# Row normalisations moved from VectorE to ScalarE, with a bias term made by GpSimd, and new instruction orders

## What is computed

```python
h = _layernorm(x) * (1 + ca) + sa              # block 0
x = x + ga * linear_attention(h)               # 16 heads of 8, elu + 1
h = _layernorm(x) * (1 + cb) + sb
xn = _layernorm(h) * gamma + beta
x = x + gb * (h + top2_of_8_experts(xn))       # 128 -> 512 -> gelu -> 128
h = _layernorm(x) * (1 + ca) + sa              # block 1
x = x + ga * softmax_attention(_layernorm(h))  # 8 heads of 16
h = _layernorm(x) * (1 + cb) + sb
x = x + gb * (h + chosen_of_8_experts(h))      # one 128 x 128 matrix each
```

## Time and profile before

| | |
|---|---|
| Median of the three runs | 684.64 us |
| Lowest and highest of them | 679.55 and 1851.92 us |
| The profiled execution's own time | 681.48 us |
| Its span in the profile | 679.7 us |
| Mean granted TensorE clock | 0.978 |
| PE busy | 607.0 us (89%), 3838 matmuls |
| DVE busy | 494.6 us (73%), 1298 instructions |
| ACT busy | 388.1 us (57%), 859 |
| POOL busy | 329.9 us (49%), 363 |
| DMA | 106.42 MB, mean 157 GB/s |

### The profile page before, as it was taken

The page is one execution under the profiler, slowest core; times in us unless marked ns, Lnnn a source line. Parts: engine busy times, 40 slices in busy tenths (PEclk is TensorE's granted clock), DMA queues, the critical chain, the costliest instruction groups (busy, mean ns, idle before and its releaser), DMA issues. The chain is left out here.

```text
span 679.7 us, 12016 instructions
## 1 busy us (share of the span) xinstructions
PE 607.0 (89%) x3838; PEld 386.7 (57%) x3838; DVE 494.6 (73%) x1298; ACT 388.1 (57%) x859; POOL 329.9 (49%) x363
## 2 busy tenths in 40 slices
PE   8889899999898899789999998888998987999974
PEld 4556558889888788566245598332344324533332
DVE  4778889931686635677868843898998872889897
ACT  2334136888656567347788666665665475555610
POOL 5203378155277767521883431448265464054623
PEclk9999999999899999989999999998999999879999
DMA  8300315777789986986488776118321829321012
GB/s 334 114 0 1 108 44 176 238 231 229 233 268 307 311 291 215 276 272 150 156 198 251 177 270 230 43 40 197 65 32 47 152 77 203 106 63 46 17 31 63
DMA packets 47422, 106.42 MB, mean 157 GB/s; under 512 B 7440, under 2 KB 22608, under 8 KB 45824
## 3 DMA queue, kind: packets, MB, share of 16 engines
q1 hardware_dynamic: 41808, 94.82, 47.1%
q0 software_dynamic: 5120, 10.50, 5.4%
q10 hardware_dynamic: 432, 0.34, 0.2%
...
## 5 line engine op out<-in xcount | busy, mean ns | idle before, releaser
L874 ACT ACTIVATE bufa<-PS 128x512 f32<-128x512 f32 x256 | 140.8, 599 | 68.0 <-PE PS L1565 58.2
L1206 DVE TENSOR_REDUCE mxs<-PS 128x2 f32<-128x1024 f32 x128 | 151.7, 1220 | 38.3 <-PE PS L1549 37.3
L833 ACT ACTIVATE bufb<-PS,bufb 128x128 f32<-128x128 f32 x368 | 103.5, 382 | 52.5 <-PE PS L1514 52.1
L1514 PE MATMUL PS<-bufb 128*128 128x128 f32 x736 | 98.8, 282 | 15.9 <-ACT bufb L841 6.2
L1514 PEld LDWEIGHTS PS<-bufb 128*128 128x128 f32 x736 | 90.9, 195 | 25.1 <-issue 10.7
L1522 PE MATMUL PS<-bufb 128*128 128x128 f32 x736 | 95.5, 276 | 1.5 <-ACT bufb L833 1.5
L689 POOL DMA_INDIRECT slots_in<-bufb x64 | 65.1, 1017 | 61.1 <-DVE bufb L1152 42.7
L1522 PEld LDWEIGHTS PS<-bufb 128*128 128x128 f32 x736 | 89.2, 192 | 5.7 <-ACT bufb L833 3.5
L1565 PE MATMUL PS<-stk 108*128 108x512 bf16 x256 | 85.1, 391 | 8.1 <-ACT bufa L874 6.4
L1549 PE MATMUL PS<-stk 96*128 96x512 bf16 x256 | 80.4, 402 | 7.8 <-DVE mxs L1206 4.8
L700 POOL DMA_INDIRECT bufb<-slots_out,bufb x64 | 62.4, 976 | 48.4 <-issue 33.3
...
## 6 DMA issues: line engine op xcount, KB each, us to landing
...
```

The costliest lines, as they stand in the source:

```text
L833: last = nc.scalar.activation(hs[:, n % HR, fc, :], ps[:, P * fc:P * fc + P], ACT.Gelu_apprx_tanh, bias=ws[:, n % WR, F + fc:F + fc + 1])
L874: nc.scalar.activation(probs[:, i % PR, j, :], psum("s2", i, j), ACT.Exp, scale=DH1 ** -0.5)\
L1206: nc.vector.tensor_reduce(mxs[:, gr % 2, 2 * j:2 * j + 2, h], psum("s1", i, j).rearrange("p (c n) -> p c n", c=2), axis=AX.X, op=ALU.max)\
L1514: last = nc.tensor.matmul(ps[:, P * fc:P * fc + P], ws[:, n % WR, P * fc:P * fc + P], xq[:, q % 2, P * x:P * x + P], start=True, stop=True)
```

## The change

Each `normalise` becomes a ScalarE activation, `Identity(x * scale + bias)`, with scale = `rstd` and bias = -mean * `rstd`. The mean is kept negated (a factor -0.5 in place of 0.5), and GpSimd makes the bias by one multiply more after the power. VectorE's statistics of the next pair now wait for ScalarE's normalisation of this one.

```diff
-            own.count(nc.gpsimd.memset(scales[:, :, 0], 0.5))
+            own.count(nc.gpsimd.memset(scales[:, :, 0], -0.5))
...
-                    tt(d, d, mhalf[:, :], ALU.pow).then_inc(rstd_ready[kind], 1)
+                    own.link(tt(d, d, mhalf[:, :], ALU.pow))
+                    tt(m[:, :, 0], m[:, :, 0], d, ALU.mult).then_inc(rstd_ready[kind], 1)
...
+            def normalise(kind, i, src, dst, done, lo=0, hi=NT):
+                n = NORMS.index(kind)
+                a.wait_ge(rstd_ready[kind], i + 1)
+                for t in range(lo, hi):
+                    last = nc.scalar.activation(dst[:, t, :], src[:, t, :], ACT.Identity, bias=mom[:, n, t, 0:1],
+                                                scale=rstd[:, n, t:t + 1])
+                last.then_inc(done, 1)
...
+                if kind == "an2":
+                    if i:
+                        a.wait_ge(a_oT, i)
+                        a.wait_ge(a_x, i)
+                    normalise("an1", i, tiles(X, i), za, a_z)
+                if kind == "bnn":
...
+                    normalise("bn1", i, tiles(X, i), hb[i], b_n)
+                if kind == "bn4":
+                    if i:
+                        a.wait_ge(sc_out, 256 * i)
+                    normalise("bn3", i, hb[i], z2, b_z)
...
                 if i:
-                    v.wait_ge(rstd_ready[kind], i)
+                    v.wait_ge(normed[kind], i)
...
-                own.count(nc.vector.tensor_scalar(m[:, :, 0], m[:, :, 0], 0.5, None, ALU.mult))
+                own.count(nc.vector.tensor_scalar(m[:, :, 0], m[:, :, 0], -0.5, None, ALU.mult))
...
-            def normalise(kind, i, src, dst, done, lo=0, hi=NT):
-                n = NORMS.index(kind)
-                v.wait_ge(rstd_ready[kind], i + 1)
-                if kind in OWN_NORMS:
-                    own.wait()
-                for t in range(lo, hi):
-                    last = nc.vector.tensor_scalar(dst[:, t, :], src[:, t, :], mom[:, n, t, 0:1],
-                                                   rstd[:, n, t:t + 1], ALU.subtract, ALU.mult)
...
+            normed = {"an1": a_z, "bn1": b_n, "bn3": b_z, "cn1": c_n2, "cn3": c_z, "dn1": d_z}
...
-                    normalise("bn1", i, tiles(X, i), h, None)
+                    v.wait_ge(b_n, i + 1)
```

The steps an2, bn4, cn2, cn4, dn2 and dl2 go from DVE's list to ACT's, and `bnn` is new there. All five lists are also written out in another order; two lines of POOL's show the kind of difference:

```diff
-        bga.3.0 bga.3.1 bga.3.2 bga.3.3 cn1.3.0 fin.0.0 cn2.3.0 dn1.0.0 cn3.3.0 dmo.0.0 fin.1.0 dn1.1.0 dmo.1.0 cpt.6.0 rsc.0.0
-        rsc.0.1 rsc.0.2 rsc.0.3 cpt.7.0 fin.2.0 dn1.2.0 rga.0.0 rga.0.1 dx.2.0 rga.0.2 dx.2.2 rga.0.3 dx.2.4 dx.2.6 en1.0.0
+        bga.3.0 bga.3.1 bga.3.2 bga.3.3 cn1.3.0 fin.0.0 cn2.3.0 dn1.0.0 cn3.3.0 dmo.0.0 cpt.6.0 fin.1.0 dn1.1.0 cpt.7.0 dmo.1.0
+        rsc.0.0 rsc.0.1 rsc.0.2 rsc.0.3 fin.2.0 dn1.2.0 rga.0.0 rga.0.1 rga.0.2 rga.0.3 dx.2.0 en1.0.0 dx.2.2 dx.2.4 dx.2.6
```

335 lines of the change are left out of this document (161 added, 174 removed).

## The result

| | before | changed |
|---|---|---|
| median of 3 runs | 684.64 us | 693.07 us |
| lowest and highest | 679.55 and 1851.92 us | 686.93 and 696.73 us |
| the profiled execution | 681.48 us | 693.07 us |
| its span | 679.7 us | 691.3 us |

The changed kernel is slower by a little, clear of the interval though less than 2%: 1.0166 of before, 95% interval 1.0107 to 1.0225. A second measurement (after_b) gave 1.0154 (1.0112 to 1.0196), 694.72 against 685.3 us. The forecast was 677 us, a gain of 1.1%.

The account below looks back on a forecast made before the run. TensorE was taken to bound the middle, a chain of small steps over all engines the start, VectorE the tail. Profiled 681.5 + 3 - 7 - 2 = 675.5, plus 2 for unnamed gaps, gave 677 us, range 664 to 694.

Parts of the forecast that it names:

- The start: Up to the first expert tile: about +3 us, range 0 to +6, with that tile near 109.5.
- (a) to (c): Start: slower bnn.0 step 0.8 us plus multiply 0.3; statistics about 5 us late; `z2` step 1.1 more, ending near 64.
- I count half of the delay back: Start: VectorE's list holds four steps less, 8.6 us, so half of `z2`'s almost 6 us delay returns; scatter near 82.
- (b), the place of the statistics: Start: VectorE does phi(q) of pair 1 ahead of pair 0's statistics, which start about 5 us late.
- (a) The store: Middle: store byo.2.1 goes ahead of nine stack loads, removing TensorE's 5.39 us gap before 290.75; -5.5 us with some clock.
- rival 3: Nothing gained from the moved DMAs, as bandwidth limits transfers and the gap comes elsewhere: 684.5 us, chance 0.28.
- (b) cpt.7.0: Middle, last layer's first slots: terms go before the scatter; -3.5 of 5 us, 2.0 clock and 3 gap.
- (c) Steps among the exponentials: Middle: five ScalarE steps each stall TensorE perhaps 1 us, 3 us back from sooner maxima: +2; steps before gelus covered.
- rival 1: ScalarE's in-order list blocks and each step shows on TensorE nearly in full: 27 us in the middle, 700.5 us, chance 0.12.
- (d) What no one could name: Middle: new lists may open a gap elsewhere; counted as nothing there, 6 us kept for the range.
- The tail: Last attention result to last add, VectorE busy nearly throughout: two half steps leave it; about -2 us, -4 to +1.
- three conditions for "wrong": First expert tile before 106, TensorE's waits for exponentials past 12 us in total, or a new middle gap over 4 us.

Follow-up runs that it names:

- three_moves_c: Changed kernel with pair 0's statistics before VectorE's query part, one ScalarE normalisation four gelu groups later, one expert tile's weights before nine stack loads: 695.88 us, 1.0213 of before.
- byo_only: Kernel before with one word moved, SP's store byo.2.1 ahead of the nine stack loads: 683.33 us, 1.0011 of before.
- before_dma_c: Kernel before with store byo.2.1 ahead of the nine stack loads and GpSimd's copy cpt.7.0 ahead of the 16 scatters: 697.38 us, 1.0220 of before.
- late_on_dve: Changed kernel with three attention normalisation steps (cn2.3.0, dn2.0.0, cn4.3.0) back on VectorE: 707.05 us, 1.0336 of before.
- split_only: Changed kernel's code with the orders of before, normalisations on ScalarE where VectorE had begun them: 833.45 us, 1.0591 of before, on a chip of the slower kind.
- order_only_b: Changed kernel's orders with all 25 normalisation steps back on VectorE, GpSimd still making the bias: 732.75 us, 1.0658 of before.
- mid_and_tail: Changed kernel with before's order on TensorE and VectorE between score tiles 16 and 23 and in the tail: 821.66 us, 1.0343 of before, slower kind of chip.

## Why the prediction was wrong, step by step

**The durations.** The step of 8 takes 3.18 to 3.21 us, not 2.9; the estimate of 3.2 from the Trainium skill (ScalarE: Activation LUTs, What ACT_TABLE_LOAD costs) was right and mine low. All steps fill 76.6 us of ScalarE, not 67. That its total still came to 448.6 (forecast 448) is luck: the rest of its work fills 8 us less than before. VectorE has 431.3 (forecast 444): it lost 63 us and not 51, 58.7 of them the steps, of which two were stretched (5.48 and 5.76 us), and I counted all at 2.14. The table loads are 15, as forecast. No normalisation is stretched.

**The start, +3 forecast, +5.4 at the first expert group (0 to +6 held it).** (a) to (c) were right: `z2` ends at 65.07 (forecast 64). The step that was too kind is "I count half of the delay back": 6.7 us at `z2` are still 6.2 at the scatter and 5.4 at 111.85 (in after_b 6.4, 4.0 and 4.3). three_moves_c shows that (b), the place of the statistics, was 3.3 to 4.4 us of it. In the end the start mattered less than its size: the lead that three_moves_c won there was gone by exponential 65.

**The middle, -7 forecast.** From the first gelu to the last exponential it took 535.7 us before (110.6 to 646.3) and 535.7 after (117.3 to 653.0): 0, inside -14 to +8, but made of other sums.

- (a) The store, -5.5 forecast. The cause of the gap was right (byo_only), the gain was not: a wait for the stack loads and the clock take it back (683.33 against 683.02 us). In the changed kernel the weights behind the same nine loads were late, and a gap of 5.90 us opened one tile later. This is rival 3 (its reason, the bandwidth, was not tested), and **the step that failed is to count a gap of 5.39 us as 5.5 us of gain** without asking what is late next: undone alone it gave 0 (1.0011, 0.9983 to 1.0040).
- (b) cpt.7.0, -3.5 forecast. Between exponentials 193 and 256 the change gains 8.0 us: 1.8 of the wait and the rest of it mostly clock. Before lost 7.01 x 0.28 + 9.33 x 0.07 + 9.75 x 0.25 + 9.96 x 0.09 = 6.0 us to it from 570 to 610, the change nothing. The forecast had 3.5 for the wait and the first of these four stretches. But byo_only, with the orders of before there and a wait of 2.71 us, lost only 6.94 x 0.14 + 9.45 x 0.03 + 9.46 x 0.12 + 9.81 x 0.05 = 2.9 us in the same 40 us, so some 3 of the 8 are where the falls happened to lie, and on kind B this stretch is 10 us longer with the new orders (92.1 to 93.5 against 82.0). No run takes this move alone out of the changed kernel: that it is the move's gain is likely, not shown. In the kernel before it costs: 12 us in this stretch, 15 in the whole (before_dma_c).
- (c) Steps among the exponentials, +2 forecast. They cost no more than forecast: TensorE's waits for exponentials (L1565) are 8.2 us in the whole program, 6.4 before. The 3 us that I gave back "for the maxima that come sooner" didn't come: the waits for maxima (L1549) went from 4.8 to 7.4. Yet exponentials 97 to 193 come 3.8 us sooner, and VectorE would have done worse (late_on_dve). The steps among the gelus, "covered by TensorE's lead" and put at nothing, are **the step of the middle that failed**: TensorE's waits for gelus grew by 5.9 us from the first gelu to exponential 33 (2.8 to 8.7), in a stretch that is 9.5 us longer. The 3.67 us before 239.85 are their clearest piece. Beside them stand 3.2 us more of waits for expert weights and, in return, 5.7 less for the copies and 2.1 less for slots; the rest is unused matmuls, small waits and the clock. The split alone loses 9 us there too (split_only, on kind B), but so do the orders without it (19 in order_only_b, on kind A); how the 9.5 divide between the two is not shown. It is rival 1's mechanism at a third of its price or less.
- (d) What no one could name was 4.6 us between exponentials 65 and 97, in many waits of half a microsecond, where no normalisation falls. It comes with the new order (order_only_b) and goes with the old one (mid_and_tail, on kind B).

**The tail, -2 forecast, +4.9 measured**, outside -4 to +1. ScalarE's step was as cheap as forecast: from the last of the statistics to the next transposes it is 3.4 us (666.92 to 670.32), where it was 5.2 (655.62 to 660.86). **What failed is that I put the tail down to VectorE's work alone** and did not look at fil.3.1, which the new order of TensorE puts behind a dense tile. The row order of the two lists would have shown it. With the old order there the tail is 35.9 us in place of 38.4 to 38.8 (mid_and_tail, kind B), so this place is about half of the loss; where the rest comes from is open.

So the sum is +6.7 (first gelu) + 0 + 4.9 = 11.6 us, where +3 - 7 - 2 = -6 was forecast, and +2 for the unnamed. **What went wrong in the large** is that I read the change as a split with better orders thrown in. On kind B the split alone is 5.5 to 5.9% slower, the orders alone 5.9%, and both with two or three words moved 3.8 to 4.1%; on kind A the orders alone are 6.6% slower and both together 1.5 to 1.7%. Each half is worse without the other: the orders suit this split and take a part of its cost back, at the price of two places of their own. How large that part is on kind A isn't known. No run takes back the whole 1.5%. Of my three conditions for "wrong", two stayed silent (first tile before 106, exponentials over 12 us); the third, a new gap over 4 us in the middle, came true with the 5.90 us before 303.50.
